# Spare products in TensorE's waits, and three batches of expert sums moved behind the first masked groups

## The reference, cut to what matters

```python
x = x + tanh(g_xattn[0]) * L0_xattn(layernorm(x), ctx)           # block 1: 16 heads of 64, 1601 keys
x = x + tanh(g_ffn[0]) * L0_ffn(layernorm(x), ...)               # block 2
x = x + tanh(g_xattn[1]) * L1_xattn(ctx, ctx, layernorm(x), mask)# block 3: 16 heads of 16, 1601 masked keys
x = x + tanh(g_ffn[1]) * L1_ffn(layernorm(x), ...)               # block 4: 16 heads of 16 and 8 dense experts
# inside block 2:
src = rmsnorm(src + gqa(src), norm1_w)        # attention over the batch's own 512 tokens
src = src + moe(src)                          # every token goes to 2 of 8 experts, all batches share them
out = rmsnorm(src, norm2_w)
```

## Time and profile before

| | |
|---|---|
| median of 3 runs | 3827.13 us (3823.34 to 3829.66) |
| the profiled execution | 3817.63 us, span from first to last instruction 3815.6 us |
| TensorE (PE) busy | 3487.2 us, 91% of the span |
| VectorE (DVE) busy | 1989.9 us, 52% |
| ScalarE (ACT) busy | 1435.6 us, 38% |
| GpSimd (POOL) busy | 1002.5 us, 26% |
| mean granted TensorE clock | 0.932 of full |

### The profile page before, as it was taken

One profiled execution on the slowest core, in us unless ns is written; L12 is line 12 of the kernel. 1 busy time (PEld: TensorE's weight loads), 2 busy tenths in 40 slices (PEclk: granted clock), 3 DMA queues, 4 the chain that ended last, 5 costly groups with the idle time before them and its releaser, 6 DMA issues. The chain is left out here.

```text
span 3815.6 us, 44056 instructions
## 1 busy us (share of the span) xinstructions
PE 3487.2 (91%) x18248; PEld 1464.8 (38%) x18248; DVE 1989.9 (52%) x3278; ACT 1435.6 (38%) x1639; POOL 1002.5 (26%) x481
## 2 busy tenths in 40 slices
PE   7999999989999899998786939989999999999987
PEld 3444443434434344343225702234323422343252
DVE  4444456454654546545341175555655566656444
ACT  3334344434444334443232104433454344434513
POOL 3555445364453644536301030000000000000000
PEclk9999999999999999999768959989999999999987
DMA  3000000000000000000203320101000100010000
GB/s 145 12 12 29 12 6 12 12 34 12 8 10 12 34 12 8 10 8 13 77 15 109 116 66 18 30 23 34 24 18 23 35 23 18 24 34 24 1 17 6
DMA packets 65938, 108.28 MB, mean 28 GB/s; under 512 B 4593, under 2 KB 49289, under 8 KB 65226
## 3 DMA queue, kind: packets, MB, share of 16 engines
q1 hardware_dynamic: 62666, 97.08, 8.0%
q0 software_dynamic: 3072, 8.39, 0.7%
HBM read 88.68 MB, written 16.78 MB: 28 GB/s over the span
## 5 line engine op out<-in xcount | busy, mean ns | idle before, releaser
L1451 POOL TENSOR_TENSOR wide<-wide 124x1024 f32<-124x1024 f32 (+1 forms) x352 | 828.1, 2352 | 268.1 <-ACT wide L1350 254.4
L1357 ACT ACTIVATE wide<-ring 124x1024 f32<-124x1024 f32 (+2 forms) x544 | 530.2, 1023 | 645.4 <-PE ring L1188 640.9
L1592 DVE CUSTOM_DVE_ANT_0 slim<-ring,slim 128x802 bf16<-128x802 f32 x512 | 508.6, 993 | 273.7 <-PE ring L1149 240.9
L1350 ACT ACTIVATE wide<-ring 124x1024 f32<-124x1024 f32 (+1 forms) x416 | 426.3, 1026 | 582.4 <-PE ring L1070 546.8
L1576 DVE TENSOR_REDUCE max_a<-ring 128x2 f32<-128x802 f32 x512 | 508.1, 995 | 242.5 <-PE ring L1051 242.0
L1081 PE MATMUL pv<-wide 124*64 124x512 f32 (+1 forms) x1664 | 453.2, 624 | 25.6 <-ACT wide L1350 25.6
L1070 PE MATMUL ring<-wide 64*124 64x512 f32 (+1 forms) x1664 | 429.0, 594 | 0.0
L1188 PE MATMUL ring<-slim 32*128 32x512 f32 x2176 | 403.9, 674 | 11.7 <-DVE slim L1617 7.5
L1602 DVE TENSOR_REDUCE slim<-ring 128x2 f32<-128x1024 f32 x256 | 309.3, 1223 | 190.0 <-PE ring L1161 186.9
L1465 POOL CAST slim<-slim 128x1601 bf16<-128x1601 f32 x16 | 24.6, 1538 | 1284.7 <-DMA slim<-in_ctx_k 1113.0
L1149 PE MATMUL ring<-slim 32*128 32x401 bf16 x1024 | 232.5, 358 | 47.2 <-DVE max_b L1592 34.3
(11 more groups left out here) (234 smaller groups left out, 4073.3 us busy)
## 6 DMA issues: line engine op xcount, KB each, us to landing
slim<-in_ctx_k SPq DMA_DIRECT2D x16, 800.5 KB, 4.5
wide<-in_w_pair SPq DMA_DIRECT2D x32, 384.0 KB, 3.1
slim<-in_ctx_v SPq DMA_DIRECT2D x16, 744.0 KB
wide<-in_w SPq DMA_DIRECT2D x16, 512.0 KB, 4.8
wide<-in_we SPq DMA_DIRECT2D x16, 512.0 KB, 3.5
wide<-in_ctxT SPq DMA_DIRECT2D x4, 1601.0 KB, 7.3
wide<-padded_x SPq DMA_DIRECT2D x8, 640.0 KB, 5.5
expert_rows<-wide SPq DMA_DIRECT2D x8, 640.0 KB, 3.8
```

Of the source, the lines that this page charges most:

```text
L1350: sc.activation(exps_a[0:kn, slot_of[unit], :], slot[0:kn, :], ACT.Exp, scale=WIDE ** -0.5).then_inc(scalar_done, 1)
L1357: sc.activation((exps_2 if blk == 2 else exps_34)[0:kn, first + 2 * i:first + 2 * i + 2, :].rearrange("p h n -> p (h n)"), ring_t[0:kn, ba ...
L1451: po.tensor_tensor(sums[0:kn, :], sums[0:kn, :], view, ALU.add).then_inc(pool_done, 1)
L1592: ve.tensor_tensor_reduce(out=max_junk.rearrange("p (j n) -> p j n", j=2), in0=two[:, :, 0:CHUNK], in1=maskQ_sb[:, q, c0:c0 + 2 * CHUNK].r ...
```

## The change

It has two parts. First, `Pace.accept` calls `warmed` wherever the planner expects TensorE to wait at least `WARM_FROM` = 0.8 us before a step. `warmed` emits a unit `("warm", position, count)` with one product for each 0.5 us of the expected wait less 0.3 us, at most 14. Each is a bf16 product of the identity (128x128) with 512 columns of constants into `pv_a`; nothing reads the result. They are emitted only while `pv_a` has no user: from the last `taila` of block 1 up to the first `pvb` of block 3, and after the last `tailb` of block 3. That makes 61 places with 212 products: 33 places with 110 products in the last batch of block 2 (21 of these places hold a single product), 4 with 24 around the start of block 3, and 24 with 78 in the last batch of block 4. The planner's clocks don't count them.

Second, `mix` and `rms2` of batches 1 to 3 no longer follow from a maximum of the first masked group but from `("rowb", 3, 0, b - 1)`, which stands at the start of the tiles of group b - 1.

```diff
+WARM_FROM, WARM_LESS, WARM_EACH, WARM_MOST = 0.8, 0.3, 0.5, 14
...
         if step.pe:
+            if self.spare and at - self.pe >= WARM_FROM:
+                self.spare(at - self.pe)
             self.pe = end
...
+    def warmed(idle):
+        if ("tailb", 3, B - 1, GROUPS - 1) in plan.tile_free:
+            last = ("tailb", 3, B - 1, GROUPS - 1)
+        elif ("taila", B - 1, PAIRS - 1) in plan.tile_free and ("pvb", 3, 0, 0, 0) not in plan.tile_free:
+            last = ("taila", B - 1, PAIRS - 1)
+        else:
+            return
+        emit(on(("warm", len(order), min(int((idle - WARM_LESS) / WARM_EACH), WARM_MOST)), ("scalar", last)))
...
     def mixes():
         for b in range(B):
-            yield Step(use=(("ve", 4.2),), needs=(("max3", 0, 0, b, 0, 0),) if b else (), name=("mix", b), late=3.0)
+            yield Step(use=(("ve", 4.2),), needs=(("rowb", 3, 0, b - 1),) if b else (), name=("mix", b), late=3.0)
             emit(("mix", b))
...
+    pace.spare = warmed
...
+        warm_columns = consts[:, C_STRIP:C_STRIP + S // 2].bitcast(BF16)
...
+                if kind == "warm":
+                    for lane, other in plan.tile_free[unit]:
+                        past.wait_ge(*at(lane, *other))
+                    for n in range(a[1]):
+                        pe.matmul(pv_a, ident_b[:, :], warm_columns, start=True, stop=True)
+                    continue
```

More of the change, by code:

```diff
@@ L165, in __init__ @@
         self.ring = [0.0] * RING
-        self.done, self.picked = {}, []
+        self.done, self.picked, self.spare = {}, [], None
     def start(self, step):
```

## The result

The changed kernel takes 3772.5 us (median of four runs, 3768.07 to 3790.59) against 3828.39 us before: ratio 0.9862, interval 0.9833 to 0.9892. The forecast was 3785 in a range of 3767 to 3811.

A forecast was written before the change was run, and what follows sets the result against it. TensorE, busy 91%, was taken as the bound, with VectorE bounding 78 us at block 3's start. Moved sums -9, products there -1, clock in block 2 -20 and block 4 -12 sum to -42: 3827.1 - 42 = 3785 us, range 3767 to 3811.

The forecast's parts named there:

- the disputed step: Spare products in TensorE's waits: whole-array products were taken, as likelier, to count more for the clock than narrow ones.
- the rule's rival: Only serial steps gain; block 2's groups stay at low clock and single products delay them: -21, 3806 us, 12%.
- the slower one: Rival: the products neither hold nor raise the clock and only cost time: +9, 3836 us, 5%.
- The serial steps: Block 2's last batch, steps one behind the other: 11.3 us back at full clock, times 0.8.
- the groups: Head groups of block 2's last batch: 13.3 us back, 5 for each of two slow groups, 3.3 for both others.
- the fifth that I took off: Block 2's last batch: only four fifths of 11.3 + 13.3 counted, giving 20, for doubt that the clock stays up.
- the three fifths: Block 4's last batch: three fifths of 20 counted, 12, since 1.9 and 2.7 us of waits stay without work.
- The moved sums: `mix` and `rms2` moved out of block 3's first group: -9 us in sum, bounds -20 to +5.
- 27.2 + 1: Block 3's first `rowb` comes 27.2 us sooner by the moved sums, 1 by six products ahead of it.
- 13.8 + 3.4 + 1: Given back in block 3's groups: waits at group ends +13.8, low clock behind them +3.4, square roots among exponentials +1.
- the cover: Block 3's tiles: VectorE's spare time beside them hides `mix` and `rms2`, which cost TensorE nothing; otherwise 27 us return.
- My rival for a failed cover: `rms2` keeps ScalarE's square root waiting ahead of exponentials, TensorE runs dry, 27 us return: -33, 3794 us, 8%.

The follow-up runs named there:

- narrow: The changed kernel with each spare product cut to 32 rows and 32 columns of TensorE's array, 512 streamed columns as before; ratio 0.9953.
- sums: The changed kernel with the moved sums and norms alone, no spare product anywhere; ratio 0.9959.
- ends: The changed kernel plus 20 spare products ahead of `rowb` of groups 1 to 3 of block 3's batch 0; ratio 0.9891.
- again: The changed kernel timed and profiled once more, unedited; ratio 0.9868, span 3769.7 us.
- light: The changed kernel with the planner's VectorE times for `mix` and `rms2` cut from 4.2 and 6.5 to 1.0 and 1.5 us; ratio 0.9923.
- fill: The changed kernel with one product for each 0.25 us of expected wait instead of 0.5, at most 28; ratio 0.9853.
- in_ring: The changed kernel plus 48 whole-array products in ring banks ahead of the first two tiles of block 4's head groups, batches 0 to 2; ratio 0.9842.
- in_ring_narrow: The changed kernel plus 48 products in ring banks ahead of block 4's first tiles, cut to 32 rows and 32 columns; ratio 0.9884.

## Why the prediction was right

**Whole-array products hold the clock and narrow ones hardly do.** This was the disputed step, against the rule's rival (12%) and the slower one (5%). `narrow` settles it: same places, same columns, busier engine, and the time of `sums` (0.9953 for 0.9959).

**Block 2's last batch: -20 predicted, -28.7 or -28.8 in eight of the nine profiles with the change's products, -27.9 in `ends`.** The serial steps (first `suma` to first scores, and `outb` to ranks) went from 66.2 to 56.3: 9.9 for 9.0. The term that was mis-sized is "the groups", 13.3 x 0.8 = 10.6: they went from 86.8 to 67.8, 19.0 less. The two slow groups, 24.9 and 24.7, now take 18.0 and 18.1, 6.9 and 6.6 less and not 5 each; the other two lose 2.6 and 2.8 and not 3.3 for both; and the fifth that I took off wasn't lost. But 153.0 is not the only value without whole products: the batch took 146.0 and 145.8 in `sums` and `narrow`, so the products' own effect is 22 to 29.

**Block 4's last batch: -12 predicted, -11.1** in `again` (and 2.3 less behind its last `outb`), -8.2 to -12.9 over the profiles with these products. The reason for the three fifths held: behind 2.82 and 3.12 us left empty the clock was low.

**The moved sums: -9 predicted, -13.3 to -17.2.** First turn to first `rowb`: 30.0 less in `again`, 28.8 in `sums`, for 27.2 + 1. The wait of 6.1 at each group's end came at 5.68, 5.99 and 5.80. The groups lost 12.8 to 15.5, where the sum had 13.8 + 3.4 + 1. That the cover holds depends on the maxima being held back: in `light`, where they aren't, the groups give back 28.9 for 29.1 won ahead of them. My rival for a failed cover named this outcome (-33; the ratio of `light`, 0.9923, is -29); by my sum's own terms it would have been dearer, -42 + 27 = -15, since the 18 given back at the group ends stand beside the 27.

The square roots among the exponentials cost TensorE nothing that a row shows: ScalarE's timeline of the first has 1.6 us from one load to the next.

```profile
2255.46 1.28 ACT L1327 ACT_TABLE_LOAD   x1
2256.75 0.20 ACT L1327 ACTIVATE rstd<-rstd 128x4 f32<-128x4 f32 x1
2257.06 1.28 ACT L1377 ACT_TABLE_LOAD   x1
```

**The cost of the products** was as said, nothing late at the steps of 13 and 14, and 0.23 each where I took 0.27.

**What the sum lacked** is a term of either sign for the stretches it didn't touch. In `again` they gave back 10.5. With it the profile adds up: -30.0 + 12.8 - 28.8 - 11.1 - 2.3 + 10.5 = -48.9, and with 3.1 more in stretches ahead of block 3 (1.7 before the last `suma`, 1.4 in the experts) -45.8; the spans say -45.9. The timed runs say -50 to -53 (0.9868 and 0.9862 of before). The 4 to 7 us between are not attributed. The profiled execution before was itself 10 below the median of its kernel, and that of `again` 9 above. The forecast of -42 missed by 8 to 11; the terms it had each came out larger, and the one it lacked went the other way, so that the total is as near as it is owes something to luck.

## What to carry to other kernels

Where the clock falls in waits, fill them with products that use the whole array, and size them by the true wait at full clock. Here up to 1.7 us left empty behind the products did no harm (`ends`), 2.8 and 3.1 did (`again`, block 4), and overrunning cost 3.7 in one batch (`fill`). Work that is taken out of a stretch bound by its engine comes back where that engine is late next, here at the ends of the groups; ordering it differently moved the wait into the tiles and made it dearer. Before a difference of ten us in an unedited stretch is given a cause, look whether it takes the same few values in kernels with other edits, and delay it a little to see whether it stays.

## What the hardware did that I had not expected

- **Alignment.** In the profiles that add nothing there, the same unedited stretches take from 1075.9 to 1101.8 us, with 87 to 157 us at low clock, and more of the one goes with more of the other; two profiles of the same kernel differ by 3.9. In this kernel that is larger than most edits.
- **A stall ahead of the first maximum.** In `in_ring`, `in_ring_narrow` and `ends`, which ran on one chip, VectorE starts its first masked maximum 10.0 us after TensorE's scores, in the first profile of the changed kernel 8.6; in the other ten profiles 0.5 to 0.9. All four are of kernels with both parts of the change, and six other profiles of such kernels, and `narrow`, lack it. ScalarE is late too: its copy ahead of these scores waits 3.55 us in `in_ring` and 4.15 in the first profile, with no releaser in the trace, against 1.22 in `again`. In the four profiles VectorE starts within 1.1 us of the end of the last packet of the gathers, which GpSimd issues. Timeline of VectorE and of GpSimd's last gather in `in_ring`:

```profile
2194.89 0.43 DVE L1646 CAST slim<-slim 128x512 bf16<-128x512 f32 x1 [6.36 <-issue]
2205.46 0.99 DVE L1615 CUSTOM_DVE_ANT_0 slim<-ring,slim 128x802 bf16<-128x802 f32 x1 [10.14 <-remote]
...
2202.78 0.95 POOL L1443 DMA_INDIRECT wide<-expert_rows,sources  x1 [0.30 <-issue]
```

It costs some 13 us (56.3 and 56.2 for 43.8 and 42.9) in a profiled execution. The program lets the maximum wait for the scores and for VectorE's own earlier work alone, so a link to the gathers is a guess from the times alone. What it is, and whether timed runs have it, stays open; no run tested it.
